# Scans of two rows at a time, products with B written where the states go, and two pairs of exponential buffers

## The chip, the cores and the metric

The kernel runs on one core of one Trainium2 chip. The metric is the device time of one execution in microseconds (us). Five engines take part: PE (TensorE, with its weight loads as PEld), DVE (VectorE), ACT (ScalarE), POOL (GpSimd) and SP, which issues most DMAs. Each engine works through a list of its own in order and waits on semaphores for the others.

## What is computed

Eight sequences (batches) of 512 tokens, 512 wide, go through a Mamba block and then a mixture of 8 experts, each with a residual and a layer norm. Everything is float32. The part that the change touches is the state recurrence, for 1024 inner channels d and 16 states n:

```python
dA = exp(delta[t, d] * A[d, n])
h  = h * dA + delta[t, d] * x[t, d] * B[t, n]      # 512 steps in t, h starts at 0
y[t, d] = sum over n of h[n] * C[t, n]
```

The rest of the block is a projection, a convolution of 4 taps with silu, softplus for delta, the gate, the output projection and a layer norm. Then the router sends each token to 2 of the 8 experts.

## The kernel before

The recurrence of one batch is cut into 128 steps: state n (16) by group j of 128 channels (8), `step = 8 n + j`. Channels lie on the 128 partitions and time along the row of 512 elements. Each step has three instructions, on three engines:

- ACT, `decay` (L1402 to L1410): exp into `dA[step % 2]`. These are two PSUM buffers of 128x512. It waits until the scan two steps before has read its buffer.
- POOL (L1498 to L1507): `dbu[j % 4] = u[:, j] * Bbc`, where u holds delta times x and Bbc is a row of B copied to all partitions. There are four SBUF buffers, and the instruction waits for the scan four steps before.
- DVE (L1711): the scan `h = dA * h + dbu` along the row, one instruction for each step, into `hst[n % 2][:, j]`, which holds all eight rows of a state in SBUF.

So a scan before reads one input from PSUM (dA) and one from SBUF (dbu). Before it starts it waits for its own exponential and product, and for `hT_done`, by which PE has read out state n - 2 from the same `hst` buffer.

The states go into y by parts of 128 tokens, four for each state. PE transposes eight 128x128 blocks of `hst` into `hTp` in PSUM (`state_part`, L1058), and DVE adds them, weighted by C, into y with one instruction of 128x1024 (L1541, called the sum here). Part i of state n - 1 is transposed at step j = 2i of state n and summed two steps later, the last one at step j = 0 of state n + 1.

Between the steps stand the pieces of the neighbouring batches: the expert matmuls and the output projection of the batch before, and the projection, convolution, gates and delta of the batch after. A planner puts each piece at a step of each engine's list ahead of time, from estimated costs. That order is fixed in the program and the change leaves it as it is. On POOL the pieces are elementwise products of 128x512 between SBUF buffers (L1466, L1474, L1486, L1492, L1495), and the indirect DMAs that scatter tokens (L1445) and gather results (L1460). On DVE they are the taps of the convolution (L1570), evictions and the router.

Seven of the eight batches (the main batches) run like this, from about 68 to 1918 us. The last one, called halved, goes through the states in two halves of time, with scans of 128x256 (L1719) and products of two rows in one POOL instruction (L1515). Before the first batch there is a prologue, in which delta of the first batch is added up on DVE (L1587) while POOL makes u (L1495). After the last batch there is a tail.

Of the kernel before, what the change touches and what calls it, by code (L numbers as in the profile page):

```python
# [5 lines left out]
ALU = mybir.AluOpType  # L6
ACT = mybir.ActivationFunctionType
F32 = mybir.dt.float32
# [4 lines left out]
P = 128  # L13
NB = 8
L = 512
DM = 512
DI = 2 * DM
NS = 16
# [5 lines left out]
ND = DI // P  # L24
# [14 lines left out]
NH = NT  # L39
PAIR = NT // 2  # L40
HL = L // 2
# [474 lines left out]
def build(nc, hid, hidT, w_inT, conv_w, conv_b, w_xT, w_dtT, dt_b, A_log, D, w_outT, gateT, w_expT, exp_b, ident_c, before_c, ramp_c, out):  # L516
    with ExitStack() as ctx:
        def sb(name, shape, dt=F32):
            return ctx.enter_context(nc.sbuf_tensor(name, shape, dt))

        def sem(name):
            return ctx.enter_context(nc.semaphore(name))
# [16 lines left out]
        negA = sb("negA", [P, ND, NS])  # L539
# [5 lines left out]
        rows = sb("rows", [P, L])  # L545
# [4 lines left out]
        u = [sb(f"u{s}", [P, ND, L]) for s in range(2)]  # L550
        Bbc = [sb(f"Bbc{s}", [P, L]) for s in range(2)]
        dbu = [sb(f"dbu{s}", [P, L]) for s in range(4)]
# [93 lines left out]
        def decay_of(step, halved):  # L646

            if halved:
                return dA[step // 2 % 2][:, step % 2 * HL:(step % 2 + 1) * HL]
            return dA[step % 2][:, :]  # L650


        dA = [ctx.enter_context(nc.psum_tensor(f"dA{s}", [P, L], F32)) for s in range(2)]
# [43 lines left out]
        scan_done = sem("scan_done")  # L697
        hT_done = sem("hT_done")
# [65 lines left out]
        def turned_slot(w, slot, half):  # L764

            return dA[slot][:, :] if w.seg is SEG_LAST else hTp[slot][:, half * 512:(half + 1) * 512]
# [468 lines left out]
        def _(act):  # L1235
# [166 lines left out]
            def decay(w, step):  # L1402
                n, j, halved = step // ND % NS, step % ND, w.seg.halved
                cols = slice(step // STEPS * HL, (step // STEPS + 1) * HL) if halved else slice(0, L)
                scans = max(step - 2, -1) if halved else step - 1
                if step < ND:
                    act.wait_ge(u_ready, w.b * ND + (j + 1))
                if not (w.seg is SEG_PRO and step < 2) and not (halved and step % 2):
                    act.wait_ge(scan_done, w.b * (NS * ND) + scans)
                nc.scalar.activation(decay_of(step, halved), delta[w.odd][:, j, cols], ACT.Exp, scale=negA[:, j, n:n + 1]).then_inc(exp_done, 1)  # L1410
# [19 lines left out]
        def _(pool):  # L1430
# [66 lines left out]
            def period(w):  # L1497
                for step, pieces in w.rows("pool"):  # L1498
                    n, j = step // ND, step % ND
                    if w.seg.steps and not w.seg.halved:  # L1500
                        if j == 0:
                            pool.wait_ge(b_loaded[n % 2], w.b * (16 * NS // 2) + 16 * (n // 2 + 1))
                        if n == 0:
                            pool.wait_ge(u_ready, w.b * ND + (j + 1))
                        if not (w.seg is SEG_PRO and n == 0 and j < 4):
                            pool.wait_ge(scan_done, w.b * (NS * ND) + (n * ND + j - 3))
                        nc.gpsimd.tensor_tensor(dbu[j % 4][:, :], u[w.odd][:, j, :], Bbc[n % 2][:, :], ALU.mult).then_inc(dbu_done, 1)  # L1507
                    elif w.seg.halved and j % 2 == 0:
                        k, cols = step // 2, slice(n // NS * HL, (n // NS + 1) * HL)
                        if j == 0:  # L1510
                            pool.wait_ge(b_loaded[n % 2], w.b * (16 * NS // 2) + 16 * (n // 2 + 1))
                        if n == 0:
                            pool.wait_ge(u_ready, w.b * ND + (j + 2))
                        pool.wait_ge(scan_done, w.b * (NS * ND) + (k - 3 if k < 4 else 2 * k - 6))
                        nc.gpsimd.tensor_tensor(dbu[k % 4][:, :].rearrange("p (k t) -> p k t", k=2), u[w.odd][:, j:j + 2, cols],  # L1515
                                                Bbc[n % 2][:, cols].unsqueeze(1).broadcast_to((P, 2, HL)), ALU.mult).then_inc(dbu_done, 1)
                    for x in pieces:
                        piece(w, x)
                if w.seg is SEG_PRO:
                    pool.wait_ge(xs_zeroed, 16)  # L1520
# [5 lines left out]
        def _(dve):  # L1526
            nc.vector.memset(w_rows[:, :], 0.0).then_inc(zeros_ready, 1)
# [167 lines left out]

            def period(w):
                first = w.seg is SEG_PRO
                for step, pieces in w.rows("dve"):
# [6 lines left out]
                    if w.seg.steps and not w.seg.halved:  # L1705
# [3 lines left out]
                        if not (first and n < 2):  # L1709
                            dve.wait_ge(hT_done, w.b * (NS * NH) + (n - 1) * NH)  # L1710
                        nc.vector.tensor_tensor_scan(hst[n % 2][:, j, :], dA[j % 2][:, :], dbu[j % 4][:, :], 0.0, ALU.mult, ALU.add).then_inc(scan_done, 1)  # L1711
                    elif w.seg.halved:
# [6 lines left out]
                        nc.vector.tensor_tensor_scan(hst[n % 2][:, j, start:stop], decay_of(step, True), dbu[step // 2 % 4][:, step % 2 * HL:(step % 2 + 1) * HL],  # L1719
# [55 lines left out]
```

## Time and profile before

| | |
|---|---|
| median of 3 runs | 2329.9 us (2325.55 to 2331.84) |
| the profiled execution, its own time | 2326.37 us |
| its span, first to last instruction | 2324.6 us |
| busy share of the span | PE 88%, DVE 90%, POOL 78%, ACT 65% |
| span by stage | prologue to 68 us, main batches to 1918, halved batch to about 2200, tail |

A row of the page names line, engine, operation, output<-inputs and shape, then the busy time, the mean duration of one, and the idle time of the engine just before it with what ended that idle time. In a timeline the first number is the start in us and the second the time until the end of the last of "xN" instructions; in square brackets stands the idle time before. An instruction's time begins when its engine takes it up, so a delay inside the engine is part of its duration, while a wait on a semaphore is not.

### The profile page before, as it was taken

How to read it: one execution, taken by the hardware profiler on the slowest of the kernel's cores; microseconds unless marked ns; L12 is line 12 of the kernel's file. 1: busy time of each engine (PE TensorE's matmuls, PEld its weight loads, DVE VectorE, ACT ScalarE, POOL GpSimd, SP SyncE). 2: the span in 40 equal slices, each digit the busy share in tenths (PEclk: the TensorE clock that was granted, in tenths of full speed). 3: DMA queues.
4: the chain of work that ended last, by engine and by line, in shares of the span. 5: the costliest groups of instructions: out<-in, count | busy, mean ns of one | idle time of the engine just before them, and what ended most of it. 6: DMA issues, size and time to landing. Idle time of an engine off the chain costs nothing.

```text
span 2324.6 us, 30122 instructions
## 1 busy us (share of the span) xinstructions
PE 2053.7 (88%) x8604; PEld 1206.9 (52%) x8604; DVE 2102.9 (90%) x2369; ACT 1518.4 (65%) x2748; POOL 1802.4 (78%) x1448
## 2 busy tenths in 40 slices
PE   8795779897989989899898998899898998779998
PEld 3444555555545555555555555455555555555443
DVE  5899999999999999999999999999999999899833
ACT  5757855785577765778567774778566785555411
POOL 2959997798887888879887889879888797685402
PEclk9997889898999999999999999999999999779999
DMA  5311041357543584446753576446743467575613
GB/s 171 112 42 68 19 132 59 118 187 255 158 117 137 196 285 121 127 150 227 258 127 98 180 268 207 114 152 202 273 126 109 155 226 265 138 229 178 195 68 81
DMA packets 205315, 367.94 MB, mean 158 GB/s; under 512 B 28472, under 2 KB 34744, under 8 KB 205152
## 3 DMA queue, kind: packets, MB, share of 16 engines
q1 hardware_dynamic: 186032, 331.54, 42.7%
q0 software_dynamic: 12544, 29.37, 6.0%
q10 hardware_dynamic: 6576, 5.11, 1.0%
q8 instruction: 72, 1.18, 0.2%
q14 instruction: 91, 0.75, 0.1%
HBM read 287.05 MB, written 78.91 MB: 157 GB/s over the span
## 4 chain that ended last, share of the span: by engine, by line
DVE 26%; PE 26%; POOL 23%; issue 12%; DMA 6%; ACT 4%; SPq 2%; DVEq 0%; POOLq 0%; ACTq 0%
PE bank L1044 18%; POOL dbu L1507 14%; DVE hst L1711 11%; DVE y L1541 6%; PE hTp L1058 5%; DVE u L1570 3%; POOL u L1495 3%; POOL delta L1492 3%; DVE hst L1719 3%; DMA zs<-sorted_tokens 2%; DMA ysb<-sorted_results,place 1%; DMA Bbc<-b_scratch 1%; POOL zs L1474 1%; ACT dA L1410 1%; POOL u L1466 1%
## 5 line engine op out<-in xcount | busy, mean ns | idle before, releaser
L1507 POOL TENSOR_TENSOR dbu<-u,Bbc 128x512 f32<-128x512 f32 x896 | 1144.6, 1313 | 192.9 <-DVE hst L1711 185.1
L1711 DVE TENSOR_TENSOR_SCAN hst<-dA,dbu 128x512 f32<-128x512 f32 x896 | 1053.2, 1209 | 22.0 <-ACT dA L1410 17.3
L1410 ACT ACTIVATE dA<-delta,negA 128x512 f32<-128x512 f32 (+1 forms) x1152 | 723.7, 639 | 450.4 <-DVE hst L1711 359.0
L1058 PE MATMUL hTp<-ident,hst 128*128 128x128 f32 x4096 | 561.1, 288 | 135.6 <-DVE y L1541 40.0
L1058 PEld LDWEIGHTS hTp<-ident,hst 128*128 128x128 f32 x4096 | 494.1, 149 | 356.5 <-issue 133.1
L1541 DVE SCALAR_TENSOR_TENSOR y<-hTp,Ct,y 128x1024 f32<-128x1024 f32 x512 | 647.4, 1265 | 30.5 <-PE hTp L1058 29.2
L1044 PE MATMUL bank<-wslot,hidT 128*128 128x512 f32 x512 | 244.4, 613 | 23.4 <-ACT zs L1348 17.1
L1044 PE MATMUL bank<-delta,tokT 128*128 128x512 f32 x480 | 223.9, 603 | 1.7 <-issue 1.0
L1044 PE MATMUL bank<-wslot,tokT 128*128 128x512 f32 x464 | 218.6, 601 | 5.9 <-ACT ysb L1391 3.5
L1515 POOL TENSOR_TENSOR dbu<-u,Bbc 128x512 f32<-128x512 f32 x128 | 162.8, 1310 | 74.1 <-DVE hst L1719 50.4
L1044 PE MATMUL bank<-hidT,wslot 128*128 128x512 f32 x384 | 187.8, 633 | 9.7 <-DVE u L1570 7.0
L1570 DVE SCALAR_TENSOR_TENSOR u<-bank,cw,u 128x511 f32<-128x511 f32 (+2 forms) x192 | 142.2, 743 | 29.8 <-ACT u L1281 25.0
L1044 PEld LDWEIGHTS bank<-wslot,hidT 128*128 128x128 f32 x512 | 93.8, 196 | 114.3 <-issue 90.3
L1460 POOL DMA_INDIRECT ysb<-sorted_results,place x52 | 81.4, 1565 | 84.0 <-DMA ysb<-x_scratch 74.8
L1044 PEld LDWEIGHTS bank<-wslot,tokT 128*128 128x128 f32 x464 | 82.6, 192 | 90.0 <-issue 77.7
L1044 PEld LDWEIGHTS bank<-delta,tokT 128*128 128x128 f32 x480 | 87.2, 196 | 81.0 <-issue 79.4
L1466 POOL TENSOR_TENSOR u<-u,side 128x512 f32<-128x512 f32 x64 | 81.5, 1273 | 54.7 <-ACT side L1299 54.5
L1044 PEld LDWEIGHTS bank<-hidT,wslot 128*128 128x128 f32 x384 | 72.9, 203 | 96.2 <-issue 72.3
L1495 POOL TENSOR_TENSOR u<-delta,u 128x512 f32<-128x512 f32 x64 | 81.9, 1280 | 18.7 <-DVE delta L1587 13.2
L1474 POOL TENSOR_TENSOR zs<-zs,side 128x512 f32<-128x512 f32 x64 | 87.5, 1368 | 10.6 <-ACT side L1355 10.6
L1391 ACT ACTIVATE ysb<-bank 128x512 f32<-128x512 f32 x105 | 61.6, 587 | 46.2 <-PE bank L1044 34.7
L1044 PE MATMUL bank<-wslot,side 128*128 128x512 f32 x192 | 90.7, 601 | 1.1 <-DMA wslot<-in_w_expT 0.8
(151 smaller groups left out, 2480.5 us busy)
## 6 DMA issues: line engine op xcount, KB each, us to landing
wslot<-in_w_expT SPq DMA_DIRECT2D x85, 1024.0 KB, 6.3
Bbc<-b_scratch SPq DMA_DIRECT2D x113, 256.0 KB, 3.6
zs<-sorted_tokens SPq DMA_DIRECT2D x105, 256.0 KB, 3.8
sorted_results<-ysb SPq DMA_DIRECT2D x105, 256.0 KB, 6.0
wslot<-in_w_inT SPq DMA_DIRECT2D x26, 1024.0 KB, 5.4
res<-in_w_expT SPq DMA_DIRECT2D x18, 1024.0 KB, 6.0
gate_scratch<-zs SPq DMA_DIRECT2D x64, 256.0 KB, 2.1
delta<-in_w_outT SPq DMA_DIRECT2D x14, 1024.0 KB, 10.4
```

What stands on the lines that cost most here:

```text
L1044: mm = nc.tensor.matmul(dst, lhs(k), rhs(k), start=(k == 0), stop=(k == n - 1))
L1058: mm = nc.tensor.transpose(hTp[q % 2][:, tok(j)], hst[n % 2][:, j, start:start + P], ident[:, :])
L1410: nc.scalar.activation(decay_of(step, halved), delta[w.odd][:, j, cols], ACT.Exp, scale=negA[:, j, n:n + 1]).then_inc(exp_done, 1)
L1460: nc.gpsimd.indirect_dma_start(rows_of(w, t), None, ys_dram[:, :], bass.IndirectOffsetOnAxis(ap=place[:, w.odd, t, c:c + 1], axis=0), comp ...
L1466: nc.gpsimd.tensor_tensor(x_j, x_j, side[j % 2][:, :], ALU.mult).then_inc(x_ready, 1)
L1474: nc.gpsimd.tensor_tensor(zs[i % 2][:, :], zs[i % 2][:, :], side[i % 2][:, :], ALU.mult).then_inc(z_ready, 1)
L1495: nc.gpsimd.tensor_tensor(x_j, d, x_j, ALU.mult).then_inc(u_ready, 1)
L1507: nc.gpsimd.tensor_tensor(dbu[j % 4][:, :], u[w.odd][:, j, :], Bbc[n % 2][:, :], ALU.mult).then_inc(dbu_done, 1)
L1515: nc.gpsimd.tensor_tensor(dbu[k % 4][:, :].rearrange("p (k t) -> p k t", k=2), u[w.odd][:, j:j + 2, cols], Bbc[n % 2][:, cols].unsqueeze(1 ...
L1541: nc.vector.scalar_tensor_tensor(y_part, hTp[q % 2][:, :], Ct[odd][:, t, n:n + 1], y_part, ALU.mult, ALU.add).then_inc(acc_done, 1)
L1570: tap = nc.vector.scalar_tensor_tensor(late, bank[s][:, 0:L - k], cw[:, j, TAPS - 1 - k:TAPS - k], late, ALU.mult, ALU.add)
L1711: nc.vector.tensor_tensor_scan(hst[n % 2][:, j, :], dA[j % 2][:, :], dbu[j % 4][:, :], 0.0, ALU.mult, ALU.add).then_inc(scan_done, 1)
```

## The change

Three things, in the main batches only:

1. The decays go into pairs: `dA` in PSUM is now one buffer of 2 rows, and `decay_sb` is a new one of 2 rows in SBUF. Pairs of steps take them in turn: steps j = 0, 1 and 4, 5 of every state use `dA`, and steps 2, 3 and 6, 7 use `decay_sb`. The exponential leaves out the first column of each row, which is cleared to 0 once. Its wait stands at even steps alone, for the pair four steps before.
2. The products with B of j = 0, 1 go to `first_dbu` (2 rows in SBUF), and those of j = 2 to 7 straight into the rows of `hst[n % 2]` that the scan will overwrite. POOL waits at j = 0 for the first scan pair of the state before, and at j = 2 for `hT_done` of state n - 2; it no longer waits for the scan four steps before.
3. DVE scans two rows (1024 elements) with one instruction at odd j. The decay of 0 at the second row's first column starts that row anew. The instruction waits for the exponentials and products of both rows.

The halved batch uses the same memory under new names, with decays in `dA` (PSUM) only and products in the four half buffers `first_dbu` and `decay_sb`.

```diff
-        dbu = [sb(f"dbu{s}", [P, L]) for s in range(4)]
+        first_dbu = sb("first_dbu", [P, 2, L])
+        decay_sb = sb("decay_sb", [P, 2, L])
+        half_dbu = [buf[:, k, :] for buf in (first_dbu, decay_sb) for k in range(2)]
...
+            return decay_pair(step)[:, step % 2, 1:L]
+
+        def decay_pair(step):
+
+            return decay_sb if step // 2 % 2 else dA
+
+        def dbu_row(n, j):
+
+            return first_dbu[:, j, :] if j < 2 else hst[n % 2][:, j, :]
+
+        dA = ctx.enter_context(nc.psum_tensor("dA", [P, 2, L], F32))
...
-                scans = max(step - 2, -1) if halved else step - 1
+                scans = max(step - 2, -1) if halved else step - 2
...
-                if not (w.seg is SEG_PRO and step < 2) and not (halved and step % 2):
+                if not (w.seg is SEG_PRO and step < 4) and step % 2 == 0:
                     act.wait_ge(scan_done, w.b * (NS * ND) + scans)
-                nc.scalar.activation(decay_of(step, halved), delta[w.odd][:, j, cols], ACT.Exp, scale=negA[:, j, n:n + 1]).then_inc(exp_done, 1)
+                nc.scalar.activation(decay_of(step, halved), delta[w.odd][:, j, cols if halved else slice(1, L)], ACT.Exp, scale=negA[:, j, n:n + 1]).then_inc(exp_done, 1)
...
-                        if not (w.seg is SEG_PRO and n == 0 and j < 4):
-                            pool.wait_ge(scan_done, w.b * (NS * ND) + (n * ND + j - 3))
-                        nc.gpsimd.tensor_tensor(dbu[j % 4][:, :], u[w.odd][:, j, :], Bbc[n % 2][:, :], ALU.mult).then_inc(dbu_done, 1)
+                        if j == 0 and not (w.seg is SEG_PRO and n == 0):
+                            pool.wait_ge(scan_done, w.b * (NS * ND) + ((n - 1) * ND + 2))
+                        if j == 2 and not (w.seg is SEG_PRO and n < 2):
+                            pool.wait_ge(hT_done, w.b * (NS * NH) + (n - 1) * NH)
+                        nc.gpsimd.tensor_tensor(dbu_row(n, j), u[w.odd][:, j, :], Bbc[n % 2][:, :], ALU.mult).then_inc(dbu_done, 1)
...
-                        pool.wait_ge(scan_done, w.b * (NS * ND) + (k - 3 if k < 4 else 2 * k - 6))
+                        pool.wait_ge(scan_done, w.b * (NS * ND) + (k // 2 * 6 - 6 if k < 4 else 2 * k - 6))
...
+            nc.vector.memset(dA[:, :, 0:1], 0.0).then_inc(decay_cleared, 1)
+            nc.vector.memset(decay_sb[:, :, 0:1], 0.0).then_inc(decay_cleared, 1)
...
-                    if w.seg.steps and not w.seg.halved:
+                    if w.seg.steps and not w.seg.halved and j % 2:
...
-                        if not (first and n < 2):
+                        if j == 1 and not (first and n < 2):
                             dve.wait_ge(hT_done, w.b * (NS * NH) + (n - 1) * NH)
-                        nc.vector.tensor_tensor_scan(hst[n % 2][:, j, :], dA[j % 2][:, :], dbu[j % 4][:, :], 0.0, ALU.mult, ALU.add).then_inc(scan_done, 1)
+                        nc.vector.tensor_tensor_scan(pair_rows(hst[n % 2][:, j - 1:j + 1, :]), pair_rows(decay_pair(step)[:, :, :]),
+                                                     pair_rows(first_dbu[:, :, :] if j == 1 else hst[n % 2][:, j - 1:j + 1, :]), 0.0, ALU.mult, ALU.add).then_inc(scan_done, 2)
```

## Rows read from the trace of the kernel before

**Rows 1.** Busy time by stage: us and count per engine, clock, DMA share, GB/s.

```profile
68.00:1918.00 1850.00, 1637.76 (x7084) 977.85 (x7083) 1763.27 (x1836) 1294.96 (x2247) 1574.75 (x1266) 0.94 0.49 156
580.00:1660.00 1080.00, 985.20 (x4284) 581.47 (x4283) 1023.43 (x1092) 760.67 (x1338) 917.24 (x736) 0.97 0.55 175
```

**Rows 2.** Waits, 68 to 1918 us: engine, line, releaser, total us, times, longest.

```profile
DVE y L1541 <- PE hTp L1058: 21.9, 32, 1.6
DVE hst L1711 <- ACT dA L1410: 17.3, 22, 2.0
...
POOL dbu L1507 <- DVE hst L1711: 185.1, 181, 3.3
POOL u L1466 <- ACT side L1299: 22.4, 20, 4.5
POOL y L1486 <- DMA spare<-gate_scratch: 14.9, 4, 4.6
POOL sorted_tokens L1445 <- ACT tokT L1379: 14.6, 11, 4.0
POOL zs L1474 <- ACT side L1355: 10.6, 9, 1.7
```

**Rows 3.** Scans by source line: count, then min/median/max in ns.

```profile
L1711 DVE TENSOR_TENSOR_SCAN hst<-dA,dbu x896: 1192/1211/1240, 68.9 to 1917.3; 128x512 f32<-128x512 f32 x180
L1719 DVE TENSOR_TENSOR_SCAN hst<-dA,dbu x128: 658/666/692, 1919.6 to 2068.0; 128x256 f32<-128x256 f32 x128
```

**Rows 4.** Timeline of DVE, a quiet stretch of a main batch.

```profile
1030.95 2.33 DVE L1711 TENSOR_TENSOR_SCAN hst<-dA,dbu 128x512 f32<-128x512 f32 x2
1033.20 1.26 DVE L1541 SCALAR_TENSOR_TENSOR y<-hTp,Ct,y 128x1024 f32<-128x1024 f32 x1
```

**Rows 5.** The router's small scan by source line, both inputs in SBUF.

```profile
L1653 DVE TENSOR_TENSOR_SCAN end<-ones,tiles x7: 174/175/749, 431.2 to 2021.9; 128x8 f32<-128x8 f32 x7
```

**Rows 6.** Timeline around its longest one, DVE and POOL.

```profile
429.38 2.50 POOL L1507 TENSOR_TENSOR dbu<-u,Bbc 128x512 f32<-128x512 f32 x2 [0.58 <-DVE hst L1711]
...
431.16 0.75 DVE L1653 TENSOR_TENSOR_SCAN end<-ones,tiles 128x8 f32<-128x8 f32 x1
```

**Rows 7.** A product of the router with both inputs in SBUF: source line, then timeline.

```profile
L1681 DVE TENSOR_TENSOR mix<-eg,mix x9: 160/1055/1061, 436.6 to 2260.4; 128x4 f32<-128x4 f32 x7, 128x2 f32<-128x2 f32 x2
...
992.46 1.06 DVE L1681 TENSOR_TENSOR mix<-eg,mix 128x4 f32<-128x4 f32 x1
...
992.23 1.27 POOL L1507 TENSOR_TENSOR dbu<-u,Bbc 128x512 f32<-128x512 f32 x1 [0.58 <-DVE hst L1711]
```

**Rows 8.** Timeline of the prologue, DVE and POOL.

```profile
56.29 0.68 DVE L1587 TENSOR_TENSOR delta<-delta,zs 128x512 f32<-128x512 f32 x1
56.50 1.60 POOL L1495 TENSOR_TENSOR u<-delta,u 128x512 f32<-128x512 f32 x1 [0.68 <-DVE delta L1587]
...
60.84 0.97 DVE L1587 TENSOR_TENSOR delta<-delta,spare 128x512 f32<-128x512 f32 x1 [0.98 <-ACT spare L1333]
...
60.00 1.27 POOL L1495 TENSOR_TENSOR u<-delta,u 128x512 f32<-128x512 f32 x1 [0.68 <-DVE delta L1587]
```

**Rows 9.** POOL's groups, 68 to 1918 us: busy, mean ns, idle before.

```profile
L1507 POOL TENSOR_TENSOR dbu<-u,Bbc 128x512 f32<-128x512 f32 x896 | 1144.6, 1313 | 192.9 <-DVE hst L1711 185.1 <-DMA Bbc<-b_scratch 6.6
...
L1460 POOL DMA_INDIRECT ysb<-sorted_results,place x40 | 62.6, 1566 | 6.9 <-issue 5.0 <-DMA ysb<-x_scratch 0.2
...
L1445 POOL DMA_INDIRECT sorted_tokens<-tokT,place x24 | 24.1, 1005 | 17.7 <-ACT tokT L1379 14.6 <-issue 3.1
L1445 POOL DMA_INDIRECT sorted_tokens<-zs,place x12 | 11.9, 991 | 2.7 <-issue 1.6 <-DVE hst L1711 0.9
L1445 POOL DMA_INDIRECT sorted_tokens<-spare,place x12 | 11.8, 986 | 2.7 <-issue 2.7
```

**Rows 10.** ACT's exponentials, by shape: to PSUM, and SBUF to SBUF.

```profile
L1410 ACT ACTIVATE dA<-delta,negA 128x512 f32<-128x512 f32 x896 | 612.3, 688 | 360.7 <-DVE hst L1711 359.0
...
L1331 ACT ACTIVATE hidT<-hidT 128x512 f32<-128x512 f32 x56 | 35.0, 626 | 0.0
```

More of the change, by code:

```diff
@@ L648, in decay_of @@
             if halved:
-                return dA[step // 2 % 2][:, step % 2 * HL:(step % 2 + 1) * HL]
-            return dA[step % 2][:, :]
-        dA = [ctx.enter_context(nc.psum_tensor(f"dA{s}", [P, L], F32)) for s in range(2)]
+                return dA[:, step // 2 % 2, step % 2 * HL:(step % 2 + 1) * HL]
+            return decay_pair(step)[:, step % 2, 1:L]
[4 more added lines that the diff above has]
+        dA = ctx.enter_context(nc.psum_tensor("dA", [P, 2, L], F32))
         hTp = [ctx.enter_context(nc.psum_tensor(f"hTp{s}", [P, DI], F32)) for s in range(2)]
@@ L697, in build @@
         scan_done = sem("scan_done")
+        decay_cleared = sem("decay_cleared")
         hT_done = sem("hT_done")
@@ L764, in turned_slot @@
         def turned_slot(w, slot, half):
-            return dA[slot][:, :] if w.seg is SEG_LAST else hTp[slot][:, half * 512:(half + 1) * 512]
+            return dA[:, slot, :] if w.seg is SEG_LAST else hTp[slot][:, half * 512:(half + 1) * 512]
         NCONST = 9
@@ L1513, in period @@
                             pool.wait_ge(u_ready, w.b * ND + (j + 2))
-                        pool.wait_ge(scan_done, w.b * (NS * ND) + (k - 3 if k < 4 else 2 * k - 6))
-                        nc.gpsimd.tensor_tensor(dbu[k % 4][:, :].rearrange("p (k t) -> p k t", k=2), u[w.odd][:, j:j + 2, cols],
+                        pool.wait_ge(scan_done, w.b * (NS * ND) + (k // 2 * 6 - 6 if k < 4 else 2 * k - 6))
+                        nc.gpsimd.tensor_tensor(half_dbu[k % 4].rearrange("p (k t) -> p k t", k=2), u[w.odd][:, j:j + 2, cols],
                                                 Bbc[n % 2][:, cols].unsqueeze(1).broadcast_to((P, 2, HL)), ALU.mult).then_inc(dbu_done, 1)
@@ L1694, in piece, with pair_rows @@
                     nc.vector.tensor_tensor(res[:, t, :], ps[:, :], res[:, t, :], ALU.add).then_inc(bank_taken[s], 1)
+            def pair_rows(rows):
+                return rows.rearrange("p k t -> p (k t)")
             def period(w):
                 first = w.seg is SEG_PRO
+                if first:
+                    dve.wait_ge(decay_cleared, 2)
                 for step, pieces in w.rows("dve"):
@@ L1718, in period @@
                         dve.wait_ge(hT_done, w.b * (NS * NH) + (n - 1) * (NH if n < 2 else PAIR))
-                        nc.vector.tensor_tensor_scan(hst[n % 2][:, j, start:stop], decay_of(step, True), dbu[step // 2 % 4][:, step % 2 * HL:(step % 2 + 1) * HL],
+                        nc.vector.tensor_tensor_scan(hst[n % 2][:, j, start:stop], decay_of(step, True), half_dbu[step // 2 % 4][:, step % 2 * HL:(step % 2 + 1) * HL],
                                                      hst[n % 2][:, j, kept:kept + 1] if c else 0.0, ALU.mult, ALU.add).then_inc(scan_done, 1)
```

## The prediction

> **What bounds the kernel now.** I read the busy time by stage first [rows 1]. The change touches the main batches alone, so the stretch from 68 to 1918 us counts: 1850 us for seven batches. DVE is busy for 1763.3 of them (95%), PE for 1637.8 (89%), POOL for 1574.8 (85%), ACT for 1295.0 (70%). Then the waits [rows 2]: DVE's longest are 21.9 us on PE's transposes and 17.3 us on exponentials, small beside 87 us of DVE idle in all. POOL is idle for 1850 - 1574.8 = 275 us, and 185.1 of these are waits for scans: it runs four rows ahead and then has to stop. ACT waits 359.0 us for scans too [rows 10]. The readings agree: DVE sets the pace, and POOL and ACT wait for it. But POOL's cover is thin. Once those 185 us are used up it has only some 90 us of other idle left, most of it waits on ACT, DMAs and its own issue, and then it is the bound itself.
>
> **The change part by part.**
>
> *One scan of 1024 for two of 512.* A scan of 256 takes 666 ns and one of 512 takes 1211 ns [rows 3], so a column costs (1211 - 666) / 256 = 2.13 ns and an instruction 121 ns. A scan of 1024 should take 1211 + 512 x 2.13 = 2.30 us. But two scans back to back end after 2.33 us, not 2.42, since the second is taken up before the first ends [rows 4]. The gain is 0.03 us a pair: 448 pairs (896 / 2) x 0.03 = 13 us. A pair waits for both its rows, but these are made ahead of it.
>
> The Trainium skill, "VectorE: DVE Perf Modes", section on the TRN2 errata, has a fixed cost for each instruction, 58 cycles from SBUF and 120 from PSUM, at 0.96 GHz. By that page the estimate is 60 to 125 ns a pair, and the gain 27 to 56 us. The timeline of pairs shows 30 ns; the sum goes by it.
>
> *Where the operands lie.* Before, every scan takes its decay from PSUM and its product from SBUF. After, the pairs at j = 2, 3 and 6, 7 take the decay from `decay_sb` and the product from `hst`, both in SBUF: two pairs a state, 16 states, 7 batches, 224 scans of 2.30 us. The trace of before has such a scan only at the router, with 8 columns. Of its seven the median takes 175 ns, but one takes 749 [rows 5]. That one starts at 431.16 while POOL works on a product of two SBUF rows; POOL ends at 431.88, and the scan at 431.91 [rows 6]. So it stood still until POOL was done. The 4-column product L1681 shows it again: its median is 1055 ns with POOL at work (started at 992.23, ending at 993.50; the DVE product ends at 993.52) and its shortest 160 ns [rows 7]. The prologue has the full size: a DVE sum of 512 with both inputs in SBUF takes 0.68 us, but 0.97 us when POOL's product, running since 60.00, still has to end at 61.27. It ends at 61.81, 0.54 us after POOL [rows 8]. POOL stands still in the same way: its product at 56.50 falls into a DVE sum that ends at 56.97, takes 1.60 us for 1.27, and ends at 58.10, 1.13 us after DVE's end. The present big scans, with one SBUF input, never show it: 1192 to 1240 ns for all 896, beside a POOL busy 85% of the time [rows 1, 3].
>
> So a DVE instruction with two SBUF inputs and a POOL product exclude each other for the whole instruction. The Trainium skill says the same in "SBUF — State Buffer", section "Who interferes with whom": a DVE instruction with two SBUF inputs contends with a GpSimd instruction that reads SBUF, and whoever comes second blocks until the other is done. By that rule this change slows the kernel; the trace agrees with it, in the 749 ns.
>
> *What a hold costs POOL.* A POOL product ends; the waiting scan ends 2.30 - 0.14 = 2.16 us later (0.14 is the start-up that was already behind it: 0.68 - 0.54); the next POOL product ends 1.13 us after that. That makes 3.29 us where two products in a row are about 1.24 us apart (the 2.50 us of a couple less 1.27 [rows 6, 9]), so POOL loses 2.05 us a hold. 224 x 2.05 = 459 us. POOL's work becomes 1574.8 + 459 = 2034 us in a stretch of 1850.
>
> *What a hold costs DVE.* It waits for the rest of a POOL product, between 0 and 1.27 us, on average 0.64 if POOL is always at work. 224 x 0.64 = 143 us. DVE's own work becomes 1763 - 13 + 143 = 1893 us, less than POOL's 2034. So POOL is the new bound.
>
> *The waits of the products.* POOL may run further ahead: j = 0, 1 wait for a scan six rows back, and j = 2 waits for PE's last transposes of state n - 2, which stand at row 6 of state n - 1, four to five rows before the scan that needs the product. Behind that wait are queued the products of j = 2 to 7 and POOL's pieces, and ACT's silu and softplus wait for those. A POOL that is the bound comes to that place late and finds it passed, so I take the wait at nothing, and the 185 us of waits for scans as gone. What covers it is POOL's own lateness; without that it costs up to those 185 us.
>
> *Four exponential buffers.* They remove waits of ACT, which isn't the bound, and most of the 17.3 us of DVE [rows 2]. The exponential into SBUF has no row; 626 ns (SBUF to SBUF, another scale) and 688 ns (to PSUM) bound it [rows 10], and it is one column shorter: between 448 x 62 ns = 28 us less and nothing on an engine with 555 us idle. Nothing on the path either way. The two memsets of two columns at the start and the halved batch (decays still in PSUM, one wait moved by a few scans, once) are under 1 us.
>
> **The sum.** POOL's instructions that read no rows of SBUF can run during a hold: the gathers and scatters. The gathers are 62.6 us and the scatters 24.1 + 11.9 + 11.8 us [rows 9], together 110 us. I take it that they aren't blocked, which no row shows. A hold is there 459 / 2050 = 22% of the time, which gives back 24 us: 2034 - 24 = 2010. Then POOL's other waits stay, since their releasers are ACT and DMAs: the four rows add up to 62.5 us [rows 2], with the smaller ones and issue some 82. 2010 + 82 = 2092 us for the stretch of 1850, +242. From the profiled execution's own 2326.4 us this gives 2568, and as the median of the runs shown is 3.5 us above it, **2571 us**.
>
> Bounds. Below: if DVE's waits set the pace, 1893 us of work plus its present 87 us of idle are 1980, +130: 2460. With half the lock wait it is 2390. Above: if POOL kept all its waits for scans as well, 2092 + 185 is +427: 2757. Half of that is 2665.
>
> **The rivals.**
>
> *A, no conflict for the long scans: faster.* It could be that the blocking is a matter of starting, or that a scan of 2.13 ns a column reads its second input in the gaps. Then the gain is the 13 us of the pairs, plus up to 17 us of waits for exponentials, and some slack from POOL's longer lead: 2330 - 24 = 2306. It decides if a scan from two SBUF inputs takes 2.30 us beside a busy POOL. The evenness of the present scans speaks for nothing here (one SBUF input); against it stands the router's scan, the same operation, blocked until POOL's end.
>
> *B, conflict, but DVE stays the bound.* POOL does its products ahead between the holds, and only DVE's waits for the lock count: 2390 to 2490. For it: POOL's present 275 us of idle take up part of the 459. Against: 459 is more than 275, even if all of it could be used.
>
> *C, POOL is the bound and keeps waiting too.* Two engines at 92% and more, with lists in a fixed order and short leads, lose time to each other; the wait at j = 2 is the place where it would show. From half of the 185 us on this is above 2665, up to 2757.
>
> *D, within 0.3%.* The holds would have to cancel the 24 us by chance.
>
> **How the numbers follow.** The forecast (POOL bound, 2490 to 2680) gets 0.72, B 0.10, C above 2680 0.09, A 0.07, D 0.02. The range is 2440 to 2680: it takes in the forecast's own range and most of B, some 0.80, and leaves out A, D, the rest of B, and C. A measurement of this kernel tells differences over about 0.3% from no change. Faster by more than that: 0.07 (A). Within: 0.02 (D). Slower: 0.91 (forecast, B and C).
>
> **What the changed profile would show.** The scan group splits: pairs from dA and `first_dbu` or `hst` at 2.30 us evenly, those from `decay_sb` from 2.30 up to 3.5 us, mean about 2.9, which is the lock wait inside the instruction. POOL's products: median still near 1.27 us, but a mean near 1.7 and a maximum over 3.3 us. POOL busy near 96% of the main batches (the holds count as busy), its waits for scans near nothing, and DVE waiting for dbu, 3.2 us before, by 50 us or more. The halved batch stays at its length. Even 2.30 us scans from `decay_sb` and unchanged POOL products would prove me wrong, and A right. POOL waiting on PE's transposes at L1507 for over 90 us would be C. If the scans from dA grew as well, PSUM and not the SBUF inputs would be the cause.

## The result

The changed kernel takes 2634.6 us (median of 6 runs, 2628.79 to 2638.56), against 2330.5 us before in the same comparison (6 runs, 2323.05 to 2345.26). The ratio is 1.131, with a 95% interval from 1.128 to 1.134: the change makes the kernel 304 us slower. The prediction was 2571 us, slower, between 2440 and 2680. Direction and mechanism held. The size of the loss, worked out as 242 us against the profiled execution, came out a fifth too small.

The profiled execution of the changed kernel took 2630.4 us, with a span of 2628.6. Its first halved scan starts at 2227.7 us (before: 1919.6 [rows 3]), and from there to the end are 401 us against 405. So the loss lies in the main batches, and their stretch is now 68 to 2226 us. Here is the busy time in that stretch (the columns are as in [rows 1]: PE, PEld, DVE, ACT and POOL with their counts, PE's granted clock, DMA share, GB/s), and then the scans and products by source line (count, then min/median/max in ns):

```profile
68.00:2226.00 2158.00, 1736.42 (x7092) 1029.15 (x7091) 1950.31 (x1388) 1276.22 (x2244) 1954.54 (x1266) 0.90 0.42 134
```

```profile
L1730 DVE TENSOR_TENSOR_SCAN hst<-decay_sb,hst x224: 2273/2794/13115, 72.2 to 2223.4; 128x1024 f32<-128x1024 f32 x112
L1730 DVE TENSOR_TENSOR_SCAN hst<-dA,first_dbu x112: 2270/2290/2293, 69.8 to 2209.0; 128x1024 f32<-128x1024 f32 x112
L1730 DVE TENSOR_TENSOR_SCAN hst<-dA,hst x112: 2271/2290/2292, 76.7 to 2218.4; 128x1024 f32<-128x1024 f32 x112
...
L1519 POOL TENSOR_TENSOR hst<-u,Bbc x672: 1250/1274/3308, 69.6 to 2222.0; 128x512 f32<-128x512 f32 x168
```

The scans fall into two kinds by one thing alone, where the decay comes from. From PSUM they take 2.27 to 2.29 us, all 224 of them. From SBUF they start at the same 2.27 us and go up to 13.1. The page has their busy time and mean:

```profile
L1730 DVE TENSOR_TENSOR_SCAN hst<-decay_sb,hst 128x1024 f32<-128x1024 f32 x224 | 706.3, 3153 | 29.1 <-POOL hst L1519 18.6
...
L1730 DVE TENSOR_TENSOR_SCAN hst<-dA,hst 128x1024 f32<-128x1024 f32 x112 | 255.7, 2283 | 38.3 <-POOL hst L1519 36.1
```

224 x (3.153 - 2.284) = 195 us is the time that DVE stands still inside these scans. The products of POOL, on the other side, keep their median of 1274 ns, but the longest takes 3.31 us, near the 3.29 us that the prediction gave a product with a hold (a DVE scan that keeps POOL standing) in it. POOL's busy time grew from 1574.8 [rows 1] to 1954.5 us. PE, of which the change asks no more work, is busy for 1736.4 us in place of 1637.8, at a granted clock of 0.90 in place of 0.94.

The waits of the same stretch, as in [rows 2] (engine, line, releaser, total us, times, longest):

```profile
DVE hst L1730 <- POOL hst L1519: 54.7, 41, 2.5
DVE hst L1730 <- POOL first_dbu L1519: 47.5, 20, 4.0
...
POOL zs L1484 <- ACT side L1365: 91.6, 13, 14.4
POOL hst L1519 <- PE hTp L1068: 27.2, 14, 7.7
...
ACT ysb L1401 <- PE bank L1054: 126.9, 62, 4.4
ACT lnv L1255 <- DVE mv L1564: 126.9, 33, 12.1
```

DVE now waits 102 us for products, where it waited 3 before. POOL's 185 us of waits for scans are gone (7.3 us are left, at j = 0), and it waits 91.6 us for ACT's gates (10.6 before [rows 2]). ACT waits more than before for DVE's layer-norm statistics (126.9 us against 26.7) and for PE (`ysb`: 126.9 us against 26.5).

### The profile page after: what moved, and what is told of

It reads as the page before. It is cut to its first block, busy times and chain, and to the rows that moved or that the text cites. A ratio compares the mean times of both kernels' runs of the same rounds, so it can differ in the third digit from the quotient of the medians.

```text
span 2628.6 us, 29271 instructions
## 1 busy us (share of the span) xinstructions
PE 2151.8 (82%) x8604; PEld 1258.2 (48%) x8604; DVE 2289.8 (87%) x1923; ACT 1501.0 (57%) x2748; POOL 2183.5 (83%) x1448
## 4 chain that ended last, share of the span: by engine, by line
POOL 38%; PE 19%; DVE 18%; issue 12%; ACT 6%; DMA 6%; SPq 1%; DVEq 0%; POOLq 0%; ACTq 0%
POOL hst L1519 20%; PE bank L1054 13%; DVE hst L1730 8%; POOL first_dbu L1519 6%; PE hTp L1068 4%; DVE y L1555 4%; POOL delta L1502 3%; POOL u L1505 3%; DVE hst L1739 2%; DVE u L1584 2%; DMA ysb<-sorted_results,place 2%; POOL y L1496 1%; ACT dA L1420 1%; POOL u L1476 1%; POOL sorted_tokens L1455 1%
## 5 line engine op out<-in xcount | busy, mean ns | idle before, releaser
L1519 POOL TENSOR_TENSOR hst<-u,Bbc 128x512 f32<-128x512 f32 x672 | 1025.1, 1589 | 27.7 <-PE hTp L1068 27.2
L1068 PE MATMUL hTp<-ident,hst 128*128 128x128 f32 x4096 | 604.9, 301 | 289.5 <-DVE hst L1730 144.6
L1730 DVE TENSOR_TENSOR_SCAN hst<-decay_sb,hst 128x1024 f32<-128x1024 f32 x224 | 706.3, 3153 | 29.1 <-POOL hst L1519 18.6
L1420 ACT ACTIVATE dA<-delta,negA 128x511 f32<-128x511 f32 (+1 forms) x704 | 409.0, 604 | 228.3 <-DVE hst L1730 142.6
L1519 POOL TENSOR_TENSOR first_dbu<-u,Bbc 128x512 f32<-128x512 f32 x224 | 372.1, 1718 | 7.4 <-DVE hst L1730 7.3
L1420 ACT ACTIVATE decay_sb<-delta,negA 128x511 f32<-128x511 f32 x448 | 304.6, 713 | 120.5 <-DVE hst L1730 120.2
L1730 DVE TENSOR_TENSOR_SCAN hst<-dA,first_dbu 128x1024 f32<-128x1024 f32 x112 | 255.9, 2285 | 74.1 <-POOL first_dbu L1519 47.5
L1730 DVE TENSOR_TENSOR_SCAN hst<-dA,hst 128x1024 f32<-128x1024 f32 x112 | 255.7, 2283 | 38.3 <-POOL hst L1519 36.1
L1470 POOL DMA_INDIRECT ysb<-sorted_results,place x52 | 117.6, 2261 | 84.9 <-DMA ysb<-x_scratch 75.5
L1484 POOL TENSOR_TENSOR zs<-zs,side 128x512 f32<-128x512 f32 x64 | 91.9, 1436 | 91.6 <-ACT side L1365 91.6
L1505 POOL TENSOR_TENSOR u<-delta,u 128x512 f32<-128x512 f32 x64 | 130.8, 2044 | 18.7 <-DVE delta L1601 13.2
```

The costliest lines, as they stand in the source:

```text
L1068: mm = nc.tensor.transpose(hTp[q % 2][:, tok(j)], hst[n % 2][:, j, start:start + P], ident[:, :])
L1470: nc.gpsimd.indirect_dma_start(rows_of(w, t), None, ys_dram[:, :], bass.IndirectOffsetOnAxis(ap=place[:, w.odd, t, c:c + 1], axis=0), comp ...
L1484: nc.gpsimd.tensor_tensor(zs[i % 2][:, :], zs[i % 2][:, :], side[i % 2][:, :], ALU.mult).then_inc(z_ready, 1)
L1505: nc.gpsimd.tensor_tensor(x_j, d, x_j, ALU.mult).then_inc(u_ready, 1)
L1519: nc.gpsimd.tensor_tensor(dbu_row(n, j), u[w.odd][:, j, :], Bbc[n % 2][:, :], ALU.mult).then_inc(dbu_done, 1)
L1730: nc.vector.tensor_tensor_scan(pair_rows(hst[n % 2][:, j - 1:j + 1, :]), pair_rows(decay_pair(step)[:, :, :]), pair_rows(first_dbu[:, :, : ...
```

## The experiments

The theory: a scan with both inputs in SBUF and a POOL product exclude each other, POOL loses the length of the scan and DVE the rest of the product. Its rivals were that the pairs, the new wait at j = 2, or SBUF decays as such cost the time. The expectations speak of a port: it is their word for what a scan and a product take in turn.

### Products in place, nothing else

The kernel before, with the products and POOL's waits of the change (the four rows of `dbu` become four of `first_dbu`, of which the main batches use two):

```diff
-                        if not (w.seg is SEG_PRO and n == 0 and j < 4):
-                            pool.wait_ge(scan_done, w.b * (NS * ND) + (n * ND + j - 3))
-                        nc.gpsimd.tensor_tensor(dbu[j % 4][:, :],
+                        if j == 0 and not (w.seg is SEG_PRO and n == 0):
+                            pool.wait_ge(scan_done, w.b * (NS * ND) + ((n - 1) * ND + 2))
+                        if j == 2 and not (w.seg is SEG_PRO and n < 2):
+                            pool.wait_ge(hT_done, w.b * (NS * NH) + (n - 1) * NH)
+                        nc.gpsimd.tensor_tensor(dbu_row(n, j),
```

> The kernel before with one part of the change: products with B of j = 2 to 7 go into the rows of hst, those of j = 0, 1 into two rows of their own, with the waits of the change. Decays stay in two PSUM rows and each step has its own scan, so every scan has one SBUF input. Theory (the two SBUF inputs of the scans from decay_sb shut POOL out and are shut out by it): nothing of the loss is here, the time is 2310 to 2340 us, all scans stay at 1.19 to 1.24 us. Rival (the new wait of POOL at j = 2 for PE's transposes): it is here in full, 2400 us or more, with POOL idle at the product line on PE by over 90 us. A gain from POOL's longer lead would be at most the 3 us that DVE waited for products.

Measured: 2322.1 us against 2327.7 in the same comparison, ratio 0.997 (0.9954 to 0.9985), so 5.6 us or 0.2% faster, within the expected band. Of the versions here that do the whole computation this is the fastest.

```profile
L1513 POOL TENSOR_TENSOR hst<-u,Bbc 128x512 f32<-128x512 f32 x672 | 865.2, 1355 | 41.1 <-PE hTp L1062 40.7
L1717 DVE TENSOR_TENSOR_SCAN hst<-dA,hst 128x512 f32<-128x512 f32 x672 | 789.1, 1208 | 14.4 <-ACT dA L1414 13.8
```

```profile
POOL zs L1478 <- ACT side L1359: 71.6, 20, 8.9
```

The wait at j = 2 is there (40.7 us of POOL idle) and costs nothing. The products in place and that wait are cleared of the loss. POOL's wait for ACT's gates is there too, 71.6 us of it and without any loss of time: it came as POOL's waits for scans went (185.1 us before, 17.5 here).

### The pairing undone

The changed kernel's buffers, with one scan for each step (its wait for `hT_done` moves from j = 1 to j = 0):

```diff
-                    if w.seg.steps and not w.seg.halved and j % 2:
+                    if w.seg.steps and not w.seg.halved:
...
-                        nc.vector.tensor_tensor_scan(pair_rows(hst[n % 2][:, j - 1:j + 1, :]), pair_rows(decay_pair(step)[:, :, :]),
-                                                     pair_rows(first_dbu[:, :, :] if j == 1 else hst[n % 2][:, j - 1:j + 1, :]), 0.0, ALU.mult, ALU.add).then_inc(scan_done, 2)
+                        nc.vector.tensor_tensor_scan(hst[n % 2][:, j, :], decay_pair(step)[:, j % 2, :], dbu_row(n, j), 0.0, ALU.mult, ALU.add).then_inc(scan_done, 1)
```

> The changed kernel with its pairing undone: the same buffers (two PSUM rows, two SBUF rows of decays, products in place), but one scan of 512 for each step, so 448 scans of 1.21 us have both inputs in SBUF in place of 224 of 2.30. Theory: POOL is shut out for nearly as long (448 x 0.96 = 430 us against 459), but DVE asks twice as often and waits each time; with 0.64 us a time that is 287 us in place of 143. Expected 2640 to 2760 us, and those scans at a mean of 1.8 to 2.1 us beside 1.21 for those from PSUM. Rival (the pair costs, because DVE waits for both rows and hands over to PE later): without pairs the time falls back to 2330 to 2450 us.

Measured: 2637.4 us (ratio 1.133, 1.131 to 1.136), just under the expected band.

```profile
L1730 DVE TENSOR_TENSOR_SCAN hst<-decay_sb,hst 128x512 f32<-128x512 f32 x448 | 891.3, 2020 | 9.8 <-POOL hst L1519 7.2
...
L1730 DVE TENSOR_TENSOR_SCAN hst<-dA,hst 128x512 f32<-128x512 f32 x224 | 262.5, 1203 | 0.6 <-ACT dA L1420 0.4
```

```profile
68.00:2230.00 2162.00, 1724.38 (x7096) 1015.65 (x7094) 2121.85 (x1836) 1279.53 (x2247) 1908.66 (x1266) 0.90 0.42 134
```

The whole loss is here without a pair, so the pairing isn't its cause. The scans from SBUF wait 448 x (2.020 - 1.204) = 366 us inside the instruction, against 195 us in the changed kernel, and DVE is busy or held for 98% of the stretch. The equal time comes about in another way than in the changed kernel, where DVE is at 90% and waits for POOL besides. The terms of the expectation were off on both sides: DVE's wait was 366 us where it had 287, and POOL's busy time grew by 334 us where it had 430.

### POOL's products shortened, in both kernels

In the changed kernel, and in the same way in the one before. Both kernels leave out the products of all but 8 columns and scan u in their place, so they don't compute the recurrence; a wait of SP for the products becomes one for the scans:

```diff
-                        sync.wait_ge(dbu_done, w.b * (NS * ND))
+                        sync.wait_ge(scan_done, w.b * (NS * ND))
...
-                        nc.gpsimd.tensor_tensor(dbu_row(n, j), u[w.odd][:, j, :], Bbc[n % 2][:, :], ALU.mult).then_inc(dbu_done, 1)
+                        nc.gpsimd.tensor_tensor(dbu_row(n, j)[:, 0:8], u[w.odd][:, j, 0:8], Bbc[n % 2][:, 0:8], ALU.mult).then_inc(dbu_done, 1)
...
-                                                     pair_rows(first_dbu[:, :, :] if j == 1 else hst[n % 2][:, j - 1:j + 1, :]), 0.0,
+                                                     pair_rows(u[w.odd][:, j - 1:j + 1, :]), 0.0,
```

> The changed kernel with POOL's products with B in the main batches cut to 8 of their 512 columns, so they leave most of that work out; the scans take u in their place as second input, still from SBUF. Theory: a scan from decay_sb finds POOL's port free nearly always. Expected 2280 to 2350 us, those scans at a mean of 2.30 to 2.45 us (POOL's other pieces remain), at most 30 us slower and up to 30 us faster than the same cut of the kernel before. Rival (scans from two SBUF inputs, or exponentials into SBUF, are slow by themselves): their mean stays above 2.9 us and the time above 2550 us.

> The kernel before with the same cut of POOL's products to 8 columns and u as the scans' second input (still one input from PSUM, one from SBUF). It is the base for short_products. DVE is the bound of the kernel before, so both theories expect 2290 to 2330 us here; the difference of the two kernels then tells what pairs are worth where POOL doesn't collide: 13 to 30 us less for the pairs by the durations of the scans.

Measured: 2283.4 us with pairs (ratio to the kernel before 0.980, 0.978 to 0.983) and 2297.4 us with single scans (0.987, 0.985 to 0.990).

```profile
L1730 DVE TENSOR_TENSOR_SCAN hst<-decay_sb,u 128x1024 f32<-128x1024 f32 x224 | 524.8, 2343 | 12.5 <-issue 12.5
L1730 DVE TENSOR_TENSOR_SCAN hst<-dA,u 128x1024 f32<-128x1024 f32 x224 | 510.4, 2279 | 14.9 <-issue 9.7
```

Take away most of POOL's reading, and the same scan from two SBUF inputs takes 2.34 us in place of 3.15, and the loss is gone. Scans from SBUF decays aren't slow by themselves. An exponential into SBUF takes 713 ns against 682 into PSUM (both 511 columns), in this kernel as in the changed one, and costs nothing here. With little left to collide the whole change is worth 14 us between the medians of four runs each, of which the farthest lies 9 us from its median, so the 14 is rough. How much of it is the pairs isn't shown: the products in place had brought 5.6 us in the experiment above.

### A pause between POOL's products

The trace of the changed kernel has 24 scans of more than 3.6 us, which together take 104 us more than 2.284 each. Five of them take 13.1 us, and all five start during a gather. Here is one, on DVE's and then on POOL's timeline:

```profile
1407.76 13.07 DVE L1730 TENSOR_TENSOR_SCAN hst<-decay_sb,hst 128x1024 f32<-128x1024 f32 x1
...
1407.31 1.57 POOL L1470 DMA_INDIRECT ysb<-sorted_results,place  x1 [0.16 <-issue]
1408.31 3.08 POOL L1519 TENSOR_TENSOR hst<-u,Bbc 128x512 f32<-128x512 f32 x2
1410.77 1.84 POOL L1484 TENSOR_TENSOR zs<-zs,side 128x512 f32<-128x512 f32 x1
1411.99 3.04 POOL L1519 TENSOR_TENSOR hst<-u,Bbc 128x512 f32<-128x512 f32 x2
1414.43 1.81 POOL L1484 TENSOR_TENSOR zs<-zs,side 128x512 f32<-128x512 f32 x1
1415.65 3.02 POOL L1519 TENSOR_TENSOR hst<-u,Bbc 128x512 f32<-128x512 f32 x2
```

POOL runs eight products while the scan waits. Each is recorded at 1.8 us though they start 1.22 us apart, so by the record the next one has begun before the last ends. The last ends at 1418.67, and the scan at 1420.83, 2.16 us later. A scan of 8.3 us, started at 531.18, shows that the 1.8 us aren't needed for a long wait: it waits through six products which are recorded at 1.25 to 1.27 us and start 1.23 us apart.

The edit, in the changed kernel:

```diff
+                        if w.b or step:
+                            pool.wait_ge(dbu_done, w.b * (NS * ND) + step)
                         nc.gpsimd.tensor_tensor(dbu_row(n, j), u[w.odd][:, j, :], Bbc[n % 2][:, :], ALU.mult).then_inc(dbu_done, 1)
```

> The changed kernel, with POOL waiting before each product with B until its own last product is done, so that no two products are in flight at once. In the changed kernel 24 of the 224 scans from two SBUF inputs take 3.7 to 13.1 us and together 104 us more than 2.284 us each: POOL starts up to nine products in a row beside a waiting scan. Theory (the port goes to DVE only if POOL has no product already started behind the running one): with the pause no scan waits longer than one product, none is over 3.8 us, their mean falls from 3.15 to 2.7 to 2.9 us, and the time to 2540 to 2620 us, less a cost of the pause of up to 0.1 us a product. Rival (long waits come from the gathers or from load): the scans over 3.8 us stay, and the pause makes it slower, 2640 to 2720 us.

Measured: 2634.0 us (ratio 1.131, 1.126 to 1.136), no change.

```profile
L1732 DVE TENSOR_TENSOR_SCAN hst<-decay_sb,hst x224: 2273/2697/4335, 72.9 to 2231.0; 128x1024 f32<-128x1024 f32 x112
```

```profile
L1732 DVE TENSOR_TENSOR_SCAN hst<-decay_sb,hst 128x1024 f32<-128x1024 f32 x224 | 631.2, 2818 | 42.2 <-POOL hst L1521 26.2
L1732 DVE TENSOR_TENSOR_SCAN hst<-dA,first_dbu 128x1024 f32<-128x1024 f32 x112 | 256.0, 2286 | 100.7 <-POOL first_dbu L1521 73.7
```

```profile
68.00:2235.00 2167.00, 1768.65 (x7099) 1038.67 (x7098) 1878.80 (x1389) 1276.96 (x2246) 1997.74 (x1266) 0.88 0.41 133
```

The long waits mostly went: the maximum fell from 13.1 to 4.3 us and the mean from 3.15 to 2.82, so that DVE's wait inside these scans went from 195 to 120 us. Five scans are still over the 3.8 us that none was to pass. So products sent without a pause are part of the cause of the long waits; the exact rule by which a scan gets in isn't shown. The expected time, 2540 to 2620 us and a cost of the pause of up to 0.1 us a product, would have been a gain; it didn't come. DVE waits for products instead, 140 us in place of 102, POOL is busy for 43 us more, and PE for 32 us more at a granted clock of 0.88 in place of 0.90. What the pause itself costs was priced in the kernel with a loaded POOL (below) by the same two lines:

> The kernel pool_load (POOL loaded, no conflict) with the pause of pool_pause: POOL waits before each product with B until its own last one is done. It prices the pause where POOL is close to the bound. In pool_pause the scans' waits for the port fell from 195 to 120 us and the time stayed at 2634 us. Theory 1 (the pause costs POOL what it gives DVE): 0.05 to 0.1 us a product, so 30 to 80 us over pool_load's 2460, 2490 to 2540 us. Theory 2 (POOL is the bound of the changed kernel, and DVE's waits for the port don't count): the pause is nearly free, 2455 to 2480 us.

Measured: 2494.0 us, against 2460.2 without the pause: 34 us, so the pause isn't free, as theory 1 had it. It costs some 34 us where POOL is close to the bound and spares DVE 75 us inside its scans. That these two cancel in the changed kernel is likely but not shown; they aren't equal.

### Each side's loss alone, as plain work

To the kernel with products in place comes plain work: every scan keeps one input in PSUM, and none took over 1.23 us. For POOL, every fourth step:

```diff
+                        if j % 4 == 2:
+                            nc.gpsimd.tensor_tensor(first_dbu[:, 2:4, 0:365], u[w.odd][:, j - 1:j + 1, 0:365], u[w.odd][:, j - 1:j + 1, 0:365], ALU.mult).then_inc(extra_done, 1)
```

> The kernel in_place (all scans from one PSUM and one SBUF input, no conflict) with one more POOL instruction of 2 x 365 columns for every four steps, into rows that nobody reads: 224 of about 1.7 us, 380 us, as much as POOL's busy time in the main batches grew in the changed kernel (1574.8 to 1954.5 us). It is the loss of POOL alone, without DVE's waits for the port. Theory (POOL becomes the bound): 1575 + 380 us of work and its 82 us of waits for ACT and DMAs in a stretch of 1850, so 2500 us, between 2460 and 2540. Rival (POOL's lead covers it and DVE's lock waits are the whole loss): under 2400 us.

For DVE:

```diff
+                        if j % 4 == 2:
+                            nc.vector.memset(first_dbu[:, 2:4, 0:470], 0.0).then_inc(extra_done, 1)
```

> The kernel in_place with a memset of 2 x 470 columns on DVE for every four steps, into rows that nobody reads: 224 of about 0.87 us, 195 us, as much as the scans from two SBUF inputs waited inside the instruction in the changed kernel. It is DVE's loss alone. Theory: DVE is the bound, so nearly all of it is on the path: 2500 us, between 2470 and 2530. If either load alone gave the 2630 us of the changed kernel, the other side would be free; the theory says that both sides are needed for the whole loss. Rival (DVE's waits hide behind a POOL that is the bound): this would say little here, but a time near 2630 would exclude it.

And for both, with 900 columns on POOL and, on DVE:

```diff
+                            nc.vector.tensor_reduce(first_dbu[:, 3, L - 1:L], w_rows[:, 0:730], AX.X, ALU.max).then_inc(late_done, 1)
```

(Waits of each load for the one before it are left out of the three cuts.)

> The kernel in_place with both losses of the changed kernel as plain work, free of any conflict: for every four steps one more POOL instruction of 900 columns (in pool_load 730 columns took 1.53 us and POOL's busy time grew by 299 us; the growth to match is 380, so some 170 columns more), and one more DVE reduction of 730 columns from SBUF (about 0.85 us by the memset of dve_load, 190 us in all). Alone, such loads gave 2460 (POOL) and 2479 us (DVE). Theory (the two engines wait for each other, and both losses add up nearly): 2580 to 2640 us, as the changed kernel. Rival (the sum of work isn't enough, and it is the place of the holds that costs, because a scan and a product can't run at the same time): 2500 to 2560 us, and the rest of the changed kernel's loss is that exclusion.

Measured: POOL's load alone 2460.2 us, at the lower edge of what was expected, DVE's alone 2478.7, both 2543.3 (ratios 1.057, 1.066 and 1.091, each +/- 0.005). The loads alone were short of the losses that they stand for: POOL's busy time grew by 299 us, not 380, and DVE's by 171, not 195. The loads together missed the theory's band of 2580 to 2640 us and fell into the rival's. The stretch of main batches with both:

```profile
68.00:2142.00 2074.00, 1710.15 (x7091) 1010.45 (x7089) 1973.72 (x2060) 1306.40 (x2249) 1933.12 (x1490) 0.92 0.43 139
```

With both, DVE has 1974 us of work and POOL 1933, against the 1950 and 1955 of the changed kernel, in a stretch that is 84 us shorter. So plain work of nearly the same amount gives 221 of the 312 us that separate the changed kernel from the one with products in place (2634.6 - 2322.1), and 91 us are left. POOL's load was 21 us short of its mark and DVE's 23 us over it, so the amounts don't explain the 91 us.

The rival stands: that a scan and a product can't run at the same time costs beyond the time they hold each other up. Through what isn't shown, but the traces tell where to look. With plain work on both engines ACT's two waits from above are as short as before (the first two lines below), while they are 126.9 us each in the changed kernel and as long in the kernel with single scans (the last two):

```profile
ACT lnv L1251 <- DVE mv L1564: 21.4, 27, 1.3
ACT ysb L1397 <- PE bank L1050: 12.5, 16, 1.3
...
ACT lnv L1255 <- DVE mv L1564: 144.0, 33, 11.0
ACT ysb L1401 <- PE bank L1054: 134.7, 60, 3.6
```

PE is busy for 26 us more in the changed kernel than with both loads, at a granted clock of 0.90 against 0.92. That may have a part in the 91 us, and no run separates it.

### Every third scan from SBUF

The kernel with products in place, and a third row of decays, in SBUF:

```diff
-            return dA[step % 2][:, :]
+            return (dA[0][:, :], dA[1][:, :], first_dbu[:, 2, :])[step % 3]
```

> The kernel in_place with a third row of decays, in SBUF, used in turn with the two PSUM rows: single scans of 512, of which every third (some 299 of 896) has both inputs in SBUF, against 0 in in_place (2322 us) and 448 in single_scans (2637 us, DVE at work or waiting inside its instructions for 98% of the main batches). Theory (each scan from two SBUF inputs waits for the running product, and DVE is the bound): 299 waits of 0.8 us are 240 us, of which DVE's present idle takes some; 2510 to 2560 us, near two thirds of the way. Rival (POOL's 193 us of waits for scans absorb the holds up to a threshold): POOL loses 299 x 0.96 = 287 us, of which 193 are free, so 2400 to 2440 us.

The exponential of a step waits for the scan three steps before. Measured: 2507.9 us (ratio 1.078, 1.074 to 1.082), 2 us below the expected band and far above the rival's 2400 to 2440.

```profile
L1717 DVE TENSOR_TENSOR_SCAN hst<-dA,hst 128x512 f32<-128x512 f32 x448 | 532.6, 1204 | 14.7 <-issue 7.9 <-ACT dA L1414 6.1
L1717 DVE TENSOR_TENSOR_SCAN hst<-first_dbu,hst 128x512 f32<-128x512 f32 x224 | 382.0, 1705 | 6.0 <-ACT first_dbu L1414 3.1 <-issue 2.8
...
L1717 DVE TENSOR_TENSOR_SCAN hst<-first_dbu 128x512 f32<-128x512 f32 x74 | 160.4, 2167 | 3.3 <-POOL first_dbu L1513 1.2 <-issue 1.1 <-ACT first_dbu L1414 0.8
```

298 scans from SBUF cost 186 us over the kernel with products in place, 0.62 us each; the 448 of the kernel without pairs cost 315, 0.70 each. So POOL's idle time doesn't soak up the holds of 298 scans. With two counts alone it isn't shown that the first few cost as much.

## Why the prediction was right, and where its size was off

*What bounds the kernel, and the conflict.* Right. That DVE sets the pace before is borne out in the kernel with products in place: 171 us more work of DVE make it 157 us slower. That scans from `decay_sb` and POOL's products exclude each other was read from a scan of 8 columns, a product of 4 and the prologue's sum of 512 [rows 5 to 8]. It holds for 1024 columns in full: 2.27 to 2.29 us from PSUM, 2.27 to 13.1 from SBUF, and 2.34 on average once POOL's products are short. The Trainium skill's rule ("SBUF — State Buffer", section "Who interferes with whom") spoke against this change, and the runs agree: the mean of 3.15 us becomes 2.34 when POOL hardly reads. By that rule the one that comes second waits until the other is done; here the trace differs, since five scans waited through eight products.

*The pair.* The term was 13 us, 0.03 us a pair, and too small: DVE's busy time in scans would fall from 1053 to 448 x 2.284 = 1023 us, by 30. That the medians of the kernels with short products differ by 14 doesn't confirm the 13, since they differ in the whole change. The pair (2.284 us) lies some 0.05 to 0.07 us under two single scans in a row (2.33 us [rows 4], 2.35 on average). The Trainium skill's fixed costs of an instruction in "VectorE: DVE Perf Modes" (section on the TRN2 errata), 60 to 125 ns by the prediction's estimate, are at most just reached.

*What a hold costs POOL.* Too large: 459 us, where POOL's busy time grew by 380, or 1.70 us a hold in place of 2.05. The times inside a hold were right: the long scans end 2.15 to 2.16 us after POOL (2.16 in the sum), and the longest product takes 3.31 us (3.29). But the term took POOL to be always at work when the scan started, which it isn't; that this is the whole difference isn't shown. The 24 us that the sum gave back rested on gathers and scatters that run during a hold, which no row had shown, and the trace speaks against it. The 40 gathers of the main batches take 98.8 us in place of 62.6, one of them up to 3.4 us, and the 48 scatters 59.6 in place of 47.9; with both loads and no holds the gathers stay at 62.7. The gathers of the changed kernel:

```profile
L1470 POOL DMA_INDIRECT ysb<-sorted_results,place x40 | 98.8, 2470 | 7.0 <-issue 6.0
```

*What a hold costs DVE.* Too small: 143 us, where it was 195. The sum gave every scan the rest of one product, 0.64 us. For the 200 scans under 3.6 us that was rather too much: they wait 0.45 us on average (90 us). The other 24 wait through more than one instruction of POOL, up to eight, and have 104 us of it. The prediction had 3.5 us as the longest.

*POOL as the bound, with its other waits kept.* This is the step that failed most. The sum had POOL at work or held for 2010 us and idle for 82 us, 96% busy; it is busy for 1955 us and idle for 203, or 91%. So 55 us too much work and 121 us too little idle make the 66 us by which the stretch came out too short (2092 against 2158). Among the 203 are the 91.6 us of waits for ACT's gates, but they aren't by themselves the cause: the same wait is 71.6 us in the kernel with products in place, which loses nothing, and 10.0 us with the pause, which is as slow as the changed kernel. No engine is the bound by itself. Each load alone costs 138 (POOL) and 157 us (DVE) over the kernel with products in place, both together 221, and the changed kernel, with the exclusion in place of plain work, 312. A sum made for one engine, with the others' waits carried over from before, has no term for that. That the total came within a fifth is in part luck: the holds were too large in it and the idle too small. Rival C named this loss of two engines to each other, but put its place at the wait for PE at j = 2, which has 27.2 us and costs nothing in the experiment that has it alone.

*The waits of the products, the exponential buffers, the halved batch.* Mostly as said: 7.3 us of POOL's waits for scans are left, and the stretch from the halved batch on is 4 us shorter. The wait at j = 2, taken at nothing, is 27.2 us of POOL idle. The exponential into SBUF takes 713 ns, outside the 626 to 688 that were to bound it, on an engine with time to spare. What the two extra buffers are worth no run shows by itself.

*The rivals.* A (no conflict) fell by the first profile. B (DVE the bound) is what the kernel with single scans shows, but not this one. D (no change) is far from the measured 13%.

Open: through which waits the last 91 us come, and whether PE's lower clock has a part in them. The number of holds was varied, their place in the order of work wasn't.

## What to carry to other kernels

Before an operand of a DVE instruction moves from PSUM to SBUF, count the SBUF tensor inputs: with two of them the scans here and POOL's products took turns, and a scan that became 0.05 us cheaper cost 0.87 us more. A small instruction whose duration varies by the length of a POOL operation is the sign of it in the trace of before. When two engines at 85 to 95% hold each other up, price the loss of both, not that of the one that becomes the bound: the measured loss was 304 us, where the sum for one engine gave 242. A wait that grew in the profile isn't yet the loss: POOL's wait for ACT's gates had grown by 61 us in a kernel that was no slower.

## What the runs showed of the hardware that was not expected

The turn isn't taken fairly. A waiting scan mostly gets in after the running product (200 of 224, with waits of up to 1.3 us), but a row of POOL products without a gap can keep it out: 13.1 us for a scan of 2.28, past eight products whose starts are 1.22 us apart. In all 24 scans of more than 3.6 us the scan ends 2.15 to 2.16 us after the last product that it waited for. With POOL made to finish each product with B before it starts the next, the longest fell to 4.3 us. Which scans get in at once and which don't wasn't found, nor why products after a gather are recorded at 1.8 us each, in place of 1.27. POOL's gathers are held up like its products: 2.47 us on average in place of 1.57 in the main batches.
